# The last edge pass of a two-layer graph network: paired query rows, keys added on TensorE, sums column by column under a mask

## What is computed

```
k_j = k[src] + e          # e = edge_attr @ We, one row of 256 for each edge
v_j = v[src] + e
alpha = sum(q[dst] * k_j, axis=-1) / sqrt(C)     # 8 heads of C = 32
amax = segment_max(alpha, dst); ex = exp(alpha - amax[dst]); denom = segment_sum(ex, dst)
out = segment_sum(v_j * (ex / denom[dst])[:, :, None], dst) + x @ Ws + bs
```

## Time and profile before

| | us |
|---|---|
| median of 3 runs | 6701.87 (6700.6 to 6702.98) |
| the profiled execution, its own time | 6697.52 |
| its span | 6695.8 |
| edge pass, first instruction to end of its last | about 3927 to 6076 |

### The profile page before, as it was taken

How to read it: one execution, slowest core, us unless ns; L and a number is a source line. 1 busy time by engine, 2 the same in 40 slices (tenths; PEclk the granted TensorE clock), 3 DMA queues, 4 the chain that set the end, 5 groups by cost and what they waited for, 6 DMA issues and landing times. The chain is left out here.

```text
span 6695.8 us, 50461 instructions
## 1 busy us (share of the span) xinstructions
PE 2757.8 (41%) x11768; PEld 2050.8 (31%) x11768; DVE 4503.2 (67%) x8404; ACT 2044.1 (31%) x2631; POOL 3586.1 (54%) x3623
## 2 busy tenths in 40 slices
PE   4613100000000002458885855555555554553677
PEld 3512100000000001345553334444444444442446
DVE  3647777863544555763333559999999999997562
ACT  2013323321333332212221114444444444442220
POOL 0167767766777775413112037777777777774000
PEclk9555555555555555659998977777777777776788
DMA  2123443332533333122222157787787777882113
GB/s 81 45 72 106 138 130 106 107 89 74 201 112 110 108 108 86 47 97 101 77 69 79 66 172 247 243 250 246 243 248 246 246 246 245 248 249 83 34 44 133
DMA packets 294261, 942.07 MB, mean 141 GB/s; under 512 B 88606, under 2 KB 129443, under 8 KB 252576
## 3 DMA queue, kind: packets, MB, share of 16 engines
q0 software_dynamic: 168624, 457.37, 24.0%
q1 hardware_dynamic: 125504, 483.21, 21.3%
HBM read 625.95 MB, written 326.14 MB: 142 GB/s over the span
## 5 line engine op out<-in xcount | busy, mean ns | idle before, releaser
L1237 PE MATMUL e_psE<-e_we,e_eaT 128*128 128x256 f32 x3136 | 910.5, 461 | 918.2 <-ACT e_eaT L1180 906.6
L1104 POOL DMA_INDIRECT e_q<-q,e_idx x784 | 772.1, 985 | 558.3 <-issue 285.9
L1237 PEld LDWEIGHTS e_psE<-e_we,e_eaT 128*128 128x128 f32 x3136 | 735.9, 238 | 1076.7 <-ACT e_eaT L1180 936.9
L1108 POOL DMA_INDIRECT e_kv<-kv,e_idx x784 | 815.3, 1040 | 238.9 <-issue 235.9
L793 POOL DMA_INDIRECT g_g<-t,rec x784 | 777.0, 991 | 279.9 <-issue 279.6
L793 POOL DMA_INDIRECT g_g<-t,dst_of x784 | 740.4, 944 | 259.6 <-issue 258.0
L1164 DVE TENSOR_TENSOR_SCAN e_wv<-e_fx,e_wv 128x288 f32<-128x288 f32 x784 | 518.8, 733 | 0.0
L1341 PE MATMUL j_psM<-ident,tail 128*128 128x128 f32 x32 | 7.4, 424 | 1207.5 <-PEq L53 1207.5
L829 DVE TENSOR_TENSOR_SCAN g_wv<-g_fx,g_wv 128x2176 f32<-128x2176 f32 x98 | 459.0, 4683 | 0.4 <-issue 0.4
L804 DVE TENSOR_TENSOR g_at<-g_g,ar 128x64 f32<-128x64 f32 x98 | 26.4, 270 | 628.5 <-DMA g_g<-t,dst_of 460.6
L1204 ACT ACTIVATE e_st<-e_wv 128x2048 f32<-128x2048 f32 x98 | 379.0, 3867 | 0.0
(11 more groups left out here) (461 smaller groups left out, 6899.6 us busy)
## 6 DMA issues: line engine op xcount, KB each, us to landing
state<-e_st SPq DMA_DIRECT2D x98, 1088.0 KB, 4.7
e_ea<-in_edge_attr SPq DMA_DIRECT2D x98, 896.0 KB, 8.5
state_f<-g_st SPq DMA_DIRECT2D x49, 1088.0 KB
state_b<-g_st SPq DMA_DIRECT2D x49, 1088.0 KB
m_work<-xs SPq DMA_DIRECT2D x119, 128.0 KB, 2.2
ys<-m_work SPq DMA_DIRECT2D x119, 128.0 KB, 1.7
xs<-g_zeros SPq DMA_DIRECT2D x28, 512.0 KB
g_g<-t,rec POOLq DMA_INDIRECT x784, 2.6
```

Source lines behind the costliest of these rows:

```text
L1104: pool.indirect_dma_start(q[:, u, j, :], None, c.q, at_(j, 0)).then_inc(gat[u], 16)
L1108: pool.indirect_dma_start(kv[:, u, j, :], None, c.kv, at_(j, 1)).then_inc(gat[u], 16)
L1237: last = nc.tensor.matmul(psE[m][:, j * D:(j + 1) * D], eaT[:, m, j, k, :], we[:, k, :], start=(k == 0), stop=(k == 1))
```

## The change

1. `layer1_tables` gives each node that has edges a rank in order of its number, and scatters its q row twice, to the slots 2 rank + 1 and 2 rank + 2 of a table of twice the length. Row pair r of that table then holds the queries of ranks r-1 and r. The scatters are indirect DMAs of POOL, 14 in a group, in place of SyncE's store. The value weights become Wv - Wk.
2. `reload_edges` counts the segments along all edges, so that each even column knows its row pair (`q_of`).
3. In the pass one gather of 2 KB pairs serves two columns (4 instead of 8). Where column 2m+1 has the target of column 2m, DVE copies that query over the second half under a mask (`alike`).
4. PE adds the gathered keys to the attribute term in PSUM, as products with the identity, and so now waits for `gat`. DVE multiplies the queries straight from PSUM; adding the same PSUM bank to V - K gives V + e.
5. The maximum is taken over the whole segment within the block (a scan forward and one backward), so no shrinking factors are needed within a block. The weighted values stay in the order of edges, and their sums go column by column with `kept` (1 where the segment goes on), written straight into `st`. The ACT work for `fx` and `st` goes.

```diff
-        idx = sb("idx", [P, U, B, 4], I32)
-        kv, q, ea = sb("kv", [P, U, B, 512]), sb("q", [P, U, B, D]), sb("ea", [P, U, B, D])
+        idx, qidx, alike = sb("idx", [P, U, B], I32), sb("qidx", [P, U, B // 2], I32), sb("alike", [P, B], I32)
+        kv, q, ea = sb("kv", [P, U, B, 512]), sb("q", [P, U, B // 2, 2 * D]), sb("ea", [P, U, B, D])
...
-        wv = sb("wv", [P, D, B1])
+        parted, parted_next = sb("parted", [P, U, H, B1]), sb("parted_next", [P, U, H, B1])
+        kept_h, kept = sb("kept_h", [P, U, H, B1]), sb("kept", [P, U, B])
+        at, mt, top, ex, cw, den = (sb(n, [P, H, B1]) for n in ("at", "mt", "top", "ex", "cw", "den"))
+        wv, before = sb("wv", [P, B, D]), sb("before", [P, D])
...
-        ngat = 2 * B * 16
+        ngat = (B + B // 2) * 16
...
-                sp.wait_ge(act_st, blk + 2)
+                sp.wait_ge(std, blk + 1)
+                sp.wait_ge(act_mt, blk + 1)
...
-                    at_ = lambda j, w: bass.IndirectOffsetOnAxis(ap=idx[:, u, j, w:w + 1], axis=0)
-                    for j in range(B):
-                        pool.indirect_dma_start(q[:, u, j, :], None, c.q, at_(j, 0)).then_inc(gat[u], 16)
+                    pairs = c.q.rearrange("(r two) d -> r (two d)", two=2)
+                    for j in range(B // 2):
+                        pool.indirect_dma_start(q[:, u, j, :], None, pairs, bass.IndirectOffsetOnAxis(
+                            ap=qidx[:, u, j:j + 1], axis=0)).then_inc(gat[u], 16)
                     pool.wait_ge(used, blk + 1)
                     c.alone(pool)
                     for j in range(B):
-                        pool.indirect_dma_start(kv[:, u, j, :], None, c.kv, at_(j, 1)).then_inc(gat[u], 16)
+                        pool.indirect_dma_start(kv[:, u, j, :], None, c.kv, bass.IndirectOffsetOnAxis(
+                            ap=idx[:, u, j:j + 1], axis=0)).then_inc(gat[u], 16)
 
...
-                    copy(sepb[:, :, 1:B1], c.sep[:, bass.ds(blk * B, B)].unsqueeze(1).to_broadcast([P, H, B]))
                     v.wait_ge(gat[u], (i + 1) * ngat)
+                    v.wait_ge(marked, blk + 1)
+                    copy(alike[:], kept[:, u, :])
+                    v.drain()
+                    for m in range(B // 2):
+                        nc.vector.copy_predicated(q[:, u, m, D:2 * D], alike[:, 2 * m + 1:2 * m + 2].to_broadcast([P, D]),
+                                                  q[:, u, m, 0:D])
+                    v.drain()
                     for m in range(4):
-                        pair = psE[m][:, :].rearrange("p (j n) -> p j n", j=2)
+                        pair = psE[m][:, :]
                         v.wait_ge(ep, blk * 4 + m + 1)
-                        tt(kv[:, u, 2 * m:2 * m + 2, 0:D], kv[:, u, 2 * m:2 * m + 2, 0:D], pair, ALU.add)
-                        tt(kv[:, u, 2 * m:2 * m + 2, D:2 * D], kv[:, u, 2 * m:2 * m + 2, D:2 * D], pair,
-                           ALU.add).then_inc(ed, 1)
-                    v.drain()
-                    for j in range(B):
-                        tt(q[:, u, j, :], kv[:, u, j, 0:D], q[:, u, j, :], ALU.mult)
+                        tt(q[:, u, m, :], pair, q[:, u, m, :], ALU.mult)
+                        tt(kv[:, u, 2 * m:2 * m + 2, D:2 * D], kv[:, u, 2 * m:2 * m + 2, D:2 * D],
+                           pair.rearrange("p (j n) -> p j n", j=2), ALU.add).then_inc(ed, 1)
                     v.drain()
...
-                    nc.vector.tensor_tensor_scan(flat(mt[:]), flat(sepb[:]), flat(at[:]), 0.0, ALU.add, ALU.max)
+                    back = lambda a: a.rearrange("p h b -> p (h b)")[:, ::-1]
+                    by_head = lambda a: a.rearrange("p (h k) -> p h k", k=C)
+                    of_head = lambda b: cw[:, :, b].unsqueeze(2).to_broadcast([P, H, C])
+                    nc.vector.tensor_tensor_scan(flat(mt[:]), flat(parted[:, u]), flat(at[:]), 0.0, ALU.add, ALU.max)
                     v.drain()
-                    tt(ex[:, 0, :, :], mt[:, :, 0:B], sepb[:, :, 1:B1], ALU.add)
-                    tt(ex[:, 1, :, :], at[:, :, 1:B1], mt[:, :, 1:B1], ALU.subtract)
+                    nc.vector.tensor_tensor_scan(back(top[:]), back(parted_next[:, u]), back(mt[:]), 0.0, ALU.add, ALU.max)
+                    v.drain()
+                    tt(ex[:], at[:], top[:], ALU.subtract).then_inc(exd, 1)
                     v.drain()
                     copy(at[:, :, 0], mt[:, :, B])
-                    tt(ex[:, 0, :, :], ex[:, 0, :, :], mt[:, :, 1:B1], ALU.subtract).then_inc(exd, 1)
                     v.wait_ge(cwd, blk + 1)
-                    nc.vector.tensor_tensor_scan(flat(den[:]), flat(cw[:, 0, :, :]), flat(cw[:, 1, :, :]), 0.0,
-                                                 ALU.mult, ALU.add).then_inc(dnd, 1)
-                    weight = lambda h: cw[:, 1, h, 1:B1].unsqueeze(2).to_broadcast([P, B, C])
-                    by_edge = wv[:, :, 1:B1].rearrange("p n b -> p b n")
-                    head = lambda h: slice(h * C, (h + 1) * C)
-                    v.wait_ge(act_st, blk + 1)
-                    for h in range(H):
-                        last = tt(by_edge[:, :, head(h)], kv[:, u, :, D + h * C:D + (h + 1) * C], weight(h), ALU.mult)
+                    for b in range(B):
+                        last = tt(by_head(wv[:, b, :]), by_head(kv[:, u, b, D:2 * D]), of_head(1 + b), ALU.mult)
                     last.then_inc(used, 1)
+                    tt(by_head(before[:]), by_head(st[:, 1 - u, B - 1, 0:D]), of_head(0), ALU.mult)
                     v.drain()
-                    copy(cw[:, 1, :, 0], den[:, :, B])
-                    v.wait_ge(fxd, blk + 1)
-
-                    for h in range(H):
-                        last = nc.vector.tensor_tensor_scan(flat(wv[:, head(h), :]), flat(fx[:, head(h), :]),
-                                                            flat(wv[:, head(h), :]), 0.0, ALU.mult, ALU.add)
+                    tt(cw[:, :, 0], cw[:, :, 0], den[:, :, B], ALU.mult)
+                    v.drain()
+                    nc.vector.tensor_tensor_scan(flat(den[:]), flat(kept_h[:, u]), flat(cw[:]), 0.0, ALU.mult,
+                                                 ALU.add).then_inc(dnd, 1)
+                    v.wait_ge(free, blk + 1)
+                    for b in range(B):
+                        last = nc.vector.scalar_tensor_tensor(
+                            out=st[:, u, b, 0:D], in0=st[:, u, b - 1, 0:D] if b else before[:], scalar=kept[:, u, b:b + 1],
+                            in1=wv[:, b, :], op0=ALU.mult, op1=ALU.add)
+                        if b < B - 1:
+                            v.drain()
                     last.then_inc(std, 1)
                     v.wait_ge(act_mt, blk + 1)
...
+            def mark_segments(blk, u):
+                at_ = bass.ds(blk * B, B)
+                to_heads = lambda a: a[:, at_].unsqueeze(1).to_broadcast([P, H, B])
+                nc.scalar.activation(parted[:, u, :, 1:B1], to_heads(c.sep), ACT.Copy)
+                nc.scalar.activation(parted_next[:, u, :, 0:B], to_heads(c.sep), ACT.Copy)
+                nc.scalar.activation(kept_h[:, u, :, 1:B1], to_heads(c.same), ACT.Copy)
+                nc.scalar.activation(kept[:, u, :], c.same[:, at_], ACT.Copy).then_inc(marked, 1)
...
-                nc.scalar.activation(cw[:, :, :, 1:B1].rearrange("p x h b -> p (x h) b"),
-                                     ex[:].rearrange("p x h b -> p (x h) b"), ACT.Exp).then_inc(cwd, 1)
-                act.wait_ge(cwd, blk + 1)
-                nc.scalar.activation(fx[:].rearrange("p (h k) b -> p h k b", k=C),
-                                     cw[:, 0, :, :].unsqueeze(2).to_broadcast([P, H, C, B1]), ACT.Copy).then_inc(fxd, 1)
...
-                nc.scalar.activation(st[:, u, :, MX:SW].rearrange("p b h -> p h b"), mt[:, :, 1:B1], ACT.Copy)
+                nc.scalar.activation(st[:, u, :, MX:SW].rearrange("p b h -> p h b"), top[:, :, 1:B1], ACT.Copy)
...
                 act.wait_ge(std, blk + 1)
-                nc.scalar.activation(wv[:, :, 0], wv[:, :, B], ACT.Copy)
-                nc.scalar.activation(st[:, u, :, 0:D], wv[:, :, 1:B1].rearrange("p n b -> p b n"),
-                                     ACT.Copy).then_inc(act_st, 1)
+                if indices:
+                    mark_segments(blk + U, u)
...
-                    def product(m):
+                    def keys_with_attributes(m):
                         pe.wait_ge(tcp, blk * 4 + m + 1)
                         pe.wait_ge(ed, blk * 4 + m + 1)
                         for j in range(2):
+                            half = psE[m][:, j * D:(j + 1) * D]
                             for k in range(2):
-                                last = nc.tensor.matmul(psE[m][:, j * D:(j + 1) * D], eaT[:, m, j, k, :], we[:, k, :],
-                                                        start=(k == 0), stop=(k == 1))
+                                nc.tensor.matmul(half, eaT[:, m, j, k, :], we[:, k, :], start=(k == 0), stop=False)
```

(71 more changed lines are left out.)

90 lines of the change are left out of this document (60 added, 30 removed).

## The result

The changed kernel takes **6777.12 us** (6773.96 to 6779.8, 4 runs) where the kernel before takes 6701.24 on the same chip: a ratio of 1.0113, 95% interval 1.01 to 1.0125. It is slower by 1.1%; the forecast was 6513. The profiled execution took 6777.77 us, its span 6776.1.

The account below looks back on a forecast made before the run. DVE and POOL were taken as both full in the edge pass, 21.56 us a block. A period of 18.7 gives -280; 6697.5 - 280 + 78 + 5 + 8 = 6508.5, forecast 6513 us, range 6445 to 6640.

Parts of the forecast that it names:

- The new chain behind it: Edge pass: DVE's bank work, gathers, landing and products form a two-block loop of 35.4 us, allowing 17.7 a block.
- the ring: Edge pass loop over two blocks, through double buffers, from DVE's last PSUM bank via gathers and products back; forecast 35.4 us.
- B: Link from DVE's last PSUM bank to the first gather: forecast 7.8 us to `used`, measured 10.3.
- C: Link from first to last gather: forecast 9.5 us for eight gathers, measured 14.1 for twelve.
- DVE's parts: DVE's work in an edge-pass block, priced part by part: sum 18.05 us, 3.2 below the kernel before.
- The tables: `layer1_tables`: scatters delay query rows of groups 2 to 6 by 9.8 us each; with clock, tail and ranks +78 us.
- Rival 2: Edge pass: gathers come late, the last landing 4 us later; chain 19.7 us a block, time 6611; chance 0.13.
- D: Link from the last gather's start to the products' start: forecast 4.1 us, measured 6.5.
- Rival 3: TensorE's products all run at the lower clock: 21.3 us, chain 21.4 a block, time 6778; chance 0.07.
- Rival 1: DVE's masked copies or value products are dearer: 6631 or about 6620 us, both 6740; chance 0.14.
- Rival 4: More is won through no waits, cheaper masked copies or hidden scatters: 6440 us; chance 0.06.
- A: Link from the products' start to DVE's last PSUM bank: forecast 14.0 us for the products, measured 13.4.

Follow-up runs that it names:

- e13: Changed kernel with PE's edge products ahead of the gathers and only four 512-column key products behind them: 6452.56 us, 0.9627 of the kernel before.
- e16: Changed kernel with the key addition back on DVE, edge products ahead of the gathers and V itself in the table: 6690.07 us, 0.9982 of the kernel before.
- e17: Changed kernel with ACT's index copies right behind the exponential, on the first kind of chip: 6655.03 us, 0.9933 of the kernel before.
- e18: Changed kernel with early index copies and key-value gathers ahead of the query gathers, first kind of chip: 6600.57 us, 0.9853 of the kernel before.
- e1: Changed kernel with ACT's index copies right behind the exponential, on the second kind of chip: 7291.03 us, 0.9564 of the kernel before.
- e9: The kernel before, unchanged, profiled on the second kind of chip: 7630.76 us, 0.9997.
- e10: Same kernel as e1, on a third chip of the second kind: 7299.84 us, 0.9562 of the kernel before.

## Why the prediction was wrong

**The step that failed** is "The new chain behind it". It let the ring begin at `used` with eight gathers: 7.8 + 9.5 + 4.1 + 14.0 = 35.4. In the kernel POOL waits for `staged` before any gather of a block, `staged` comes from ACT behind `dnd`, and the change itself moves `dnd` behind the value products. So the ring has 10.3 us where 7.8 stood, and twelve gathers (14.1) where eight stood (9.5); the last gather took 6.5 us to the consumer and not 4.1, a value that was read from one block of before, under other traffic. That is 9.5 us more; the products' link gave 0.6 back, and 44.2 / 2 = 22.1. Against a DVE block of 18.6 the chain is the bound by 3.5 us, not level with it. e13 and e16 show it by taking products out of the chain (DVE is the bound again, 18.71 and 21.22 us); e17 and e18 by shortening B and C. The prediction had the warning in hand ("every late gather will be felt") and the sign that I gave for being wrong, DVE waiting over 1.5 us a block for PE, is what the trace shows, 3.4.

One reading ahead of it was circular. That 296 gathers in 400 us are one every 1.35 us is the block period over 16, and doesn't say that POOL is full. By the earlier trace rows a gather takes 300.23 / 296 = 1.01 us and some 0.3 of issue, so 16 take 21.0 of the 21.56 us. POOL was nearly full, and the sum doesn't change.

**DVE's parts** were right. In e13's block the masked copies run 5006.85 to 5008.46, 1.61 with drain (forecast 1.5); the eight bank operations 4.97 (5.03); the nine value products 3.21 (3.2); the eight steps 4.29 (4.1); the head's conversion 0.24 I had left out. 18.6 in all for 18.05. A masked copy of 256 takes 442 ns, close to the 418 of a two-input product of that width. The parts thus came within 0.6 us in all, and e13's period of 18.71 is the forecast 18.7, but only with the chain out of the way: the changed kernel never ran at it.

**The tables** were mis-sized: +33 us for +78. The first group ends 5 us later (3723.43 against 3718.40 in the earlier trace rows), with a start 1.7 earlier; the tail from the last rows to the next load grew by 20.9 (forecast 15). But the 9.8 us in each of five groups did not come:

```profile
3764.67 0.41 DVE L2125 TENSOR_TENSOR q_qrow<-q_psO,q_b 128x256 f32<-128x256 f32 x1
```

```profile
3756.66 1.97 POOL L2071 DMA_INDIRECT q<-q_qrow,q_slots  x1 [13.88 <-DVE q_qrow L2130]
...
3774.11 0.96 POOL L2071 DMA_INDIRECT q<-q_qrow,q_slots  x1 [0.30 <-issue]
```

DVE writes the next group's first query row at 3764.67 without a wait, while POOL's scatters of the group before run until 3775.07: the permission `q_free`, which stands behind these scatters in POOL's order, was there while six of the fourteen had started in the record. From one group's end to the next it took 0 to 2.2 us more than before, 5.7 in all six.

**The rest**: `reload_edges` +5.8 (forecast 5), the pass's start +3.4 (14), and from the last scan to the end of the span -12.9, of which -9.6 up to the next stage's first instruction (forecast for the pass's end -6). With the tables' +33.3, 97 periods +52.3 and a start of the tables 1.7 earlier that is the span's +80.3.

**The rivals.** Rival 2, late gathers, is the nearest: its mechanism is part of D, but it named neither `staged` nor the twelve gathers, and its 6611 is too small. Rival 3 gave 6778, which is the measured time by accident: the products' link was 13.4, not 21.3, and the granted clock rises within the burst, from 0.50 at 5026 to 5030 us to 1.00 from 5032 on, with the burst begun at 5025.61 (the windows above). That a burst begins cold agrees with the Trainium skill (TensorE: Matmul & The Clock Gate, "HAM oscillation"); that it stays cold throughout was this rival's own assumption, and does not hold here. Rival 1 is out by DVE's parts. Rival 4's 6440 is what e13 nearly reached, with other code.

**What stays open**: why two kinds of chips differ, and so why the change costs 1.1% on one and wins 5% on the other (next section but one); and what takes back half of the earlier issue in D. The forecast was made from, and is measured against, the first kind.

## What to carry to other kernels

When work moves behind a gather, write the ring down from release to release of the buffer, with *every* semaphore in front of the first transfer and the instruction of another engine that gives it; a permission given by a third engine as an afterthought becomes part of the ring once the slack is gone. Then put ahead of the wait whatever doesn't need its data: accumulating the edge products first and the gathered keys last kept the whole saving on DVE (6452.56 us, 3.7% below before and 4.8% below the changed kernel). And price the landing of a gather under the new traffic: here it took back about half of what an earlier issue gained.

## What the hardware showed beside that

On the second kind of chip waits end long after their producer. In e1's trace the third bank's products are recorded until 5047.5 and DVE goes on at 5054.08; e1's waits in 4400 to 6000 us have this 71 times, 352.6 us in all (the name behind the arrow is not to be trusted there):

```profile
5051.04 0.95 POOL L1106 DMA_INDIRECT e_kv<-kv,e_idx  x1 [0.30 <-issue]
5054.08 0.69 DVE L1136 TENSOR_TENSOR e_q<-e_psE,e_q 128x512 f32<-128x512 f32 x1 [5.17 <-DMA c_own<-t]
```

The kernel before on such a chip (e9) shows more of it:

```profile
4959.46 8.84 PE L1237 MATMUL e_psE<-e_we,e_eaT 128*128 128x256 f32 x32 [13.62 <-issue]
4987.18 0.94 POOL L1108 DMA_INDIRECT e_kv<-kv,e_idx  x1 [0.30 <-issue]
4992.12 0.69 DVE L1130 TENSOR_TENSOR e_kv<-e_kv,e_psE 128x512 f32<-128x512 f32 x1 [15.39 <-remote]
```

The products are recorded as over at 4968.3, DVE's next addition from PSUM, the third bank's in mid-block, comes at 4992.12. Of the 65 waits of over 3 us that DVE has at this place in e1's window, 61 end between 1.9 and 2.2 us after POOL's last gather of the run ends in the record; e10 has 65 such of 66, the changed kernel on the first kind none of 11. The early index copy of e1 and e10 puts the end of that run into DVE's work on the banks in nearly every block, which goes with the long A there. Fewer gathers in longer pauses would then suffer less, which would fit the changed kernel's gain there, but no run separates it: it is a guess. On the first kind the waits in this place end 0.03 us behind the product's record. The first scatter of a group takes 1.97 us of POOL, the others 0.96. And TensorE's mean granted clock in the pass is 0.81 in the changed kernel and 0.96 in e13 (4800 to 5200 us), where PE is busy 355 us in place of 268: the block is shorter, the products with the zero matrix are new, and the 32 edge-product instructions of a block no longer stand behind the wait for the gathers.
